# Normalized attention rows turned by DMA instead of by TensorE, and state-space tables built with fewer steps

## The reference

```python
K = einsum('chn,hnl->chl', Wc, exp(dt_Lambda[..., None] * pos))     # 32 x 128 x 1024, real part
h = concatenate([K, txt], axis=1)                                   # 32 x 205 x 1024
h = h + attention(layernorm(h), wq, wk, wv, wo)   # 32 heads of 32, 8 key/value heads, causal
h = h + ffn(layernorm(h), W_base, b_base, low-rank adapters through a Fourier transform)
```

## Time and profile before

| | us |
|---|---|
| three timed runs, median (lowest to highest) | 3075.71 (3064.27 to 3079.66) |
| the profiled execution | 3082.04 |
| its span | 3080.3 |
| busy: PE, DVE, ACT, POOL | 2781.2 (90%), 1997.8 (65%), 1094.1 (36%), 1029.9 (33%) |
| busy share of PE over the steps of attention, 400 to 1800 us | 94.5 to 96% in each 100 us |

### The profile page before, as it was taken

How to read it: one execution, slowest core, us unless ns; L and a number is a source line. 1 busy time by engine, 2 the same in 40 slices (tenths; PEclk the granted TensorE clock), 3 DMA queues, 4 the chain that set the end, 5 groups by cost and what they waited for, 6 DMA issues and landing times. The chain is left out here.

```text
span 3080.3 us, 70678 instructions
## 1 busy us (share of the span) xinstructions
PE 2781.2 (90%) x27970; PEld 2030.8 (66%) x28224; DVE 1997.8 (65%) x4642; ACT 1094.1 (36%) x2362; POOL 1029.9 (33%) x1402
## 2 busy tenths in 40 slices
PE   0847799999999999999999986699999999999999
PEld 0736698989899898989898883244444444444444
DVE  8874577787787878777787865444444444444443
ACT  3331355555555555555555565211001101100110
POOL 4631254544545454554445454011101110110110
PEclk9977899999999999999999996599999999999999
DMA  5642422222222322222222223154554455455453
GB/s 179 194 116 69 103 58 78 58 75 78 57 76 60 80 58 77 69 65 77 56 76 58 69 49 144 55 122 120 129 137 123 121 133 132 118 127 137 124 122 86
DMA packets 446040, 297.32 MB, mean 97 GB/s; under 512 B 389416, under 2 KB 407976, under 8 KB 445232
## 3 DMA queue, kind: packets, MB, share of 16 engines
q1 hardware_dynamic: 445472, 282.69, 35.7%
q10 hardware_dynamic: 240, 10.09, 1.1%
HBM read 116.36 MB, written 80.61 MB: 64 GB/s over the span
## 5 line engine op out<-in xcount | busy, mean ns | idle before, releaser
L693 POOL TENSOR_SCALAR_AFFINE_SELECT p<-p 128x256 f32<-128x256 f32 (+1 forms) x768 | 334.3, 437 | 762.0 <-ACT p L720 743.6
L805 DVE TENSOR_REDUCE mx<-psS 77x2 f32<-77x410 f32 (+1 forms) x768 | 449.3, 613 | 181.9 <-PE psS L912 110.7
L930 PE MATMUL psJ<-xth,qh 128*128 128x205 f16 x2048 | 522.0, 255 | 24.9 <-DVE qsl L813 24.7
L932 PE MATMUL psJ<-xth,ql 128*128 128x205 f16 x2048 | 518.4, 253 | 0.0
L931 PE MATMUL psJ<-xtl,qh 128*128 128x205 f16 x2048 | 516.5, 252 | 0.0
L720 ACT ACTIVATE p<-psT,escale 128x410 f32<-128x410 f32 (+1 forms) x768 | 410.4, 570 | 276.2 <-PE psT L870 256.8
L698 POOL TENSOR_TENSOR pl<-p,ph 128x410 f16<-128x410 f32 (+1 forms) x512 | 447.7, 894 | 102.5 <-ACT ph L727 95.7
L1257 POOL TENSOR_TENSOR hb<-h,bias_sb 128x1024 f32<-128x1024 f32 x52 | 122.5, 2355 | 962.4 <-DVE h L1293 962.4
L1271 ACT CAST xh<-xn 128x1024 f16<-128x1024 f32 x52 | 54.4, 1045 | 967.1 <-DVE xn L1302 967.1
L1332 PE MATMUL ps5O<-woh,ath 128*128 128x512 f16 x832 | 316.2, 380 | 26.3 <-DMA atl<-al 26.3
L1293 DVE SCALAR_TENSOR_TENSOR h<-ps5O,osc,h_in 128x512 f32<-128x512 f32 x104 | 78.1, 751 | 402.4 <-PE ps5O L1334 402.4
(11 more groups left out here) (227 smaller groups left out, 5906.9 us busy)
## 6 DMA issues: line engine op xcount, KB each, us to landing
a_in<-acat SPq DMA_DIRECT2D x52, 512.0 KB, 3.8
h_in<-hcat SPq DMA_DIRECT2D x52, 512.0 KB, 4.7
qst<-qsh SPq DMA_DIRECT2D x512, 51.2 KB, 2.1
out<-y SPq DMA_DIRECT2D x51, 512.0 KB, 3.1
hcat<-ob SPq DMA_DIRECT2D x64, 256.0 KB, 4.0
xin<-hcat SPq DMA_DIRECT2D x32, 512.0 KB
acat<-ao SPq DMA_DIRECT2D x32, 512.0 KB
qst<-qsl SPq DMA_DIRECT2D x256, 51.2 KB, 2.1
```

What stands on the lines that cost most here:

```text
L693: pool.affine_select(out=v, in_=v, compare_op=ALU.is_ge, fill=0.0, base=0, pattern=[[0, v.shape[1]], [1, w]], channel_multiplier=-1).then_ ...
L805: dve.tensor_reduce(dst, v, AX.X, ALU.max).then_inc(s_read, 1)
L930: pe.matmul(ps[:, 0:S], wh[:, k, c], xth[:, par, k, :], start=k == 0, stop=False)
L932: m = pe.matmul(ps[:, 0:S], wl[:, k, c], xth[:, par, k, :], start=False, stop=k == KC - 1)
```

## The change

In attention there is no unit x any more. A step earlier than before (b = -4 to 32; the norm is that of image b+4) DVE makes the statistics in slots 1 and 2 and the root in slot 3; ACT, in slots 4 to 7, subtracts the mean and casts a piece of 512 columns to the high part `xfh`, with two activations (`high_part`); DVE makes the low part `xfl` from it in slots 6, 7, 7 and in slot 0 of the next step (`low_part`). In that next step SP issues four DMA transposes (`turn`) of 128 and 80 rows, behind m of slot 0, or in step -1 behind the 17 loads. The loads and stores of rows move from SP's queue to ACT's; the store goes in two halves of 512 columns. DVE's division by the row sums is made for both tiles in one reciprocal and one product.

In the state-space stage the sizes are made by 36 small activations on ACT instead of two products on POOL; two phases are formed by DVE instead of four by ACT, the others come from an absolute value; all four products with the size are DVE's; and no channel's two products are added ahead of the matmul (16 matmuls a chunk).

```diff
--- before.py
+++ after.py
...
-            pool.wait_ge(ab_ok, 1)
-            for k in range(2):
-                pool.tensor_tensor(size[:, k], per_row(a[:]), per_step(iqr[:, k, :]), ALU.mult).then_inc(size_arg, 1)
-            pool.wait_ge(size_ok, 1)
-            for t in range(2):
-                pool.wait_ge(sine_ok, t + 1)
-                pool.tensor_tensor(tab[:, t], tab[:, t], size[:, 0], ALU.mult).then_inc(tab_ab, 1)
...
+            act.wait_ge(ab_ok, 1)
+            for k in range(2):
+                for r in range(LR):
+                    m = act.activation(size[:, k, :, r], a[:], ACT.Exp, scale=iqr[:, k, r:r + 1])
+                m.then_inc(size_ok, 1)
+            for la in range(LA):
+                m = act.activation(ela[:, la, :], a[:], ACT.Exp, scale=ila[:, la:la + 1])
+            m.then_inc(la_exp_ok, 1)
             act.wait_ge(args_ok, 1)
             act.activation(ex[:], args[:, 0].rearrange("p k h -> p (k h)"), ACT.Exp).then_inc(waves_ok, 1)
             act.activation(th[:], args[:, 0].rearrange("p k h -> p (k h)"), ACT.Tanh, scale=0.5).then_inc(waves_ok, 1)
-            for t in range(4):
-                act.wait_ge(base_ok, t // 2 + 1)
-                act.activation(turned[:, t], bases[t // 2], ACT.Identity, bias=phase[:, t:t + 1]).then_inc(turned_ok, 1)
+            act.wait_ge(turns_ok, 1)
+            act.activation(trig[:], turns[:], ACT.Sin, scale=TWO_PI).then_inc(waves_ok, 1)
             act.wait_ge(la_ok, 1)
-            act.activation(ela[:], fla[:, 0], ACT.Exp).then_inc(la_exp_ok, 1)
-            act.wait_ge(size_arg, 2)
-            act.activation(size, size, ACT.Exp).then_inc(size_ok, 1)
-            act.activation(trig[:], turns[:], ACT.Sin, scale=TWO_PI).then_inc(waves_ok, 1)
-            act.wait_ge(la_ok, 2)
             act.activation(tla[:], wla[:], ACT.Sin, scale=TWO_PI).then_inc(la_sin_ok, 1)
-            for t in range(4):
-                act.wait_ge(frac_ok, t + 1)
-                act.activation(tab[:, t], turned[:, t], ACT.Sin, scale=TWO_PI).then_inc(sine_ok, 1)
+            act.wait_ge(frac_ok, 1)
+            act.activation(turned[:, 1], turned[:, 0], ACT.Abs, scale=-1.0, bias=phase[:, 0:1]).then_inc(far_ok, 1)
+            act.activation(tab[:, 1], turned[:, 0], ACT.Sin, scale=-TWO_PI, bias=lag[:, 0:1]).then_inc(sine_ok, 1)
+            act.wait_ge(far_ok, 1)
+            act.activation(tab[:, 0], turned[:, 1], ACT.Sin, scale=-TWO_PI, bias=quarter[:, 0:1]).then_inc(sine_ok, 1)
+            act.wait_ge(frac_ok, 2)
+            act.activation(turned[:, 3], turned[:, 2], ACT.Abs).then_inc(far_ok, 1)
+            act.activation(tab[:, 3], turned[:, 2], ACT.Sin, scale=TWO_PI).then_inc(sine_ok, 1)
+            act.wait_ge(far_ok, 2)
+            act.activation(tab[:, 2], turned[:, 3], ACT.Sin, scale=-TWO_PI, bias=quarter[:, 0:1]).then_inc(sine_ok, 1)
...
-            for k in range(2):
-                dve.tensor_tensor(bases[k], per_row(f[:]), per_step(iqr[:, k, :]), ALU.mult).then_inc(base_ok, 1)
...
-            for t in range(4):
-                dve.wait_ge(turned_ok, t + 1)
-                chain(dve.tensor_scalar(tab[:, t], turned[:, t], ROUND, ROUND, ALU.add, ALU.subtract))
-                dve.tensor_tensor(turned[:, t], turned[:, t], tab[:, t], ALU.subtract).then_inc(frac_ok, 1)
+            for k in range(2):
+                m = dve.tensor_tensor(bases[k], per_row(f[:]), per_step(iqr[:, k, :]), ALU.mult)
+            chain(m)
+
+            chain(dve.tensor_scalar(tab[:, 0], base, phase[:, 0:1], ROUND, ALU.add, ALU.add))
+            dve.scalar_tensor_tensor(turned[:, 0], tab[:, 0], ROUND, base, ALU.subtract,
+                                     ALU.subtract).then_inc(frac_ok, 1)
+            chain(dve.tensor_scalar(tab[:, 2], base2, ROUND, None, ALU.add))
+            dve.scalar_tensor_tensor(turned[:, 2], tab[:, 2], ROUND, base2, ALU.subtract,
+                                     ALU.subtract).then_inc(frac_ok, 1)
...
-            dve.wait_ge(size_ok, 1)
-            for t in (2, 3):
-                dve.wait_ge(sine_ok, t + 1)
-                dve.tensor_tensor(tab[:, t], tab[:, t], size[:, 1], ALU.mult).then_inc(tab_cd, 1)
-            dve.wait_ge(tab_cd, 2)
+            dve.wait_ge(size_ok, 2)
+            dve.wait_ge(sine_ok, 4)
+            for t in range(4):
+                dve.tensor_tensor(tab[:, t], tab[:, t], size[:, t // 2], ALU.mult).then_inc(tab_ok, 1)
+            dve.wait_ge(tab_ok, 4)
...
-                    m = dve.tensor_tensor(es[:, ch % 2, k].rearrange("p h (q r) -> p h q r", r=LR), fast, slow, ALU.mult)
-                chain(m)
-                dve.tensor_tensor(es[:, ch % 2, 0, 0:SUMMED], es[:, ch % 2, 0, 0:SUMMED],
-                                  es[:, ch % 2, 1, 0:SUMMED], ALU.add).then_inc(e_ok, 1)
+                    dve.tensor_tensor(es[:, ch % 2, k].rearrange("p h (q r) -> p h q r", r=LR), fast, slow,
+                                      ALU.mult).then_inc(e_ok, 1)
...
-                    last = 0 if j < SUMMED else 1
-                    for k in range(last + 1):
+                    for k in range(2):
                         m = pe.matmul(ps[n % 4][:, j % 2, :], u[:, ch % 2, j].rearrange("p a c -> p (a c)"),
-                                      es[:, ch % 2, k, j, :], start=k == 0, stop=k == last)
+                                      es[:, ch % 2, k, j, :], start=k == 0, stop=k == 1)
...
-        xth, xtl = sb("xth", [P, 2, KC, S], F16), sb("xtl", [P, 2, KC, S], F16)
+        xfh, xfl = sb("xfh", [P, 2, D], F16), sb("xfl", [P, 2, D], F16)
+        xth, xtl = sb("xth", [P, 2, KC, P + TROWS], F16), sb("xtl", [P, 2, KC, P + TROWS], F16)
-        ao = sb("ao", [P, 2, 2, D])
+        ao = sb("ao", [P, 2, 2, D // 2])
...
-                if s >= 4 and has["ln"]:
-                    row.append(("x", s - 4))
...
-            return {"att": 0 <= b < B, "last": 0 <= b - 1 < B, "max": 0 <= b + 1 < B, "qkv": 0 <= b + 2 < B, "ln": 0 <= b + 3 < B, "load": 0 <= b + 4 < B}
+            return {"att": 0 <= b < B, "last": 0 <= b - 1 < B, "max": 0 <= b + 1 < B, "qkv": 0 <= b + 2 < B, "turn": 0 <= b + 3 < B,
+                    "ln": 0 <= b + 4 < B, "load": 2 <= b + 5 < B}
...
-                if has["load"]:
-                    wait(sp, pj_filled, base)
-                    load(b + 4, par)
                 if b == -1:
                     for dst, src, arrived in ahead:
                         sp.dma_start(dst, src).then_inc(arrived, 16)
-                if has["last"]:
-                    store(b - 1, nxt)
+                if has["turn"]:
+                    wait(sp, pj_filled, base)
+                    turn(0, nxt, b + 3)
+                    turn(1, nxt, b + 3)
...
+            def turn(t, to, n):
+                r, cols = ((P, slice(0, P)), (TROWS, slice(P, P + TROWS)))[t]
+                sp.wait_ge(x_lo, 4 * n + 2 * t + 2)
+                sp.dma_start_transpose(out=xth[:, to, :, cols], in_=xfh[0:r, t, :]).then_inc(xt_in[t], 16)
+                sp.dma_start_transpose(out=xtl[:, to, :, cols], in_=xfl[0:r, t, :]).then_inc(xt_in[t], 16)
...
+            pool.memset(xfh[:, 1, :], 0.0)
+            pool.memset(xfl[:, 1, :], 0.0)
...
+            def load(b, par):
+                act.dma_start(xin[:, par, 0, :], hcat[b * S:b * S + P, :]).then_inc(x_in[par], 16)
+                act.dma_start(xin[0:TXT, par, 1, :], hcat[b * S + P:b * S + S, :]).then_inc(x_in[par], 16)
+            def store(b, half):
+                c = slice(half * D // 2, (half + 1) * D // 2)
+                act.wait_ge(norm_done, 8 * b + 4 * half + 4)
+                act.dma_start(acat[b * S:b * S + P, c], ao[:, half, 0, :]).then_inc(a_out[half], 16)
+                act.dma_start(acat[b * S + P:b * S + S, c], ao[0:TXT, half, 1, :]).then_inc(a_out[half], 16)
+            def high_part(b, par, n):
+                t, h = divmod(n, 2)
+                c, r = slice(h * D // 2, (h + 1) * D // 2), T[t]
+                x = xin[0:r, par, t, c]
+                if n == 0:
+                    act.wait_ge(ln_done, b + 5)
+                if h == 0:
+                    wait(act, xt_in[t], 32 * (b + 4))
+                act.activation(x, x, ACT.Identity, bias=nmean[0:r, t:t + 1]).then_inc(centred, 1)
+                act.wait_ge(centred, 4 * (b + 4) + n + 1)
+                act.activation(xfh[0:r, t, c], x, ACT.Copy, scale=rs[0:r, 3, t:t + 1]).then_inc(x_hi, 1)
+            act.wait_ge(cleared, 1)
+            load(0, 0)
+            load(1, 1)
...
+                    if g == 3 and has["load"]:
+                        act.wait_ge(x_lo, 4 * (b + 4))
+                        load(b + 5, 1 - par)
+                    if g == 2 and has["last"]:
+                        store(b - 1, 1)
+                    if g == 6 and has["att"]:
+                        store(b, 0)
...
+                    if g >= 4 and has["ln"]:
+                        high_part(b, par, g - 4)
...
-                dve.reciprocal(rden[:, 0, :], o[:, 0, :, HD]).then_inc(rec_done, 1)
```

(66 more changed lines are left out.)

57 lines of the change are left out of this document (21 added, 36 removed).

## The result

| | before | after |
|---|---|---|
| median of 20 runs each, us | 3080.03 | 3097.01 |
| the profiled execution, us | 3082.04 | 3101.61 |
| its span, us | 3080.3 | 3099.9 |
| granted TensorE clock, mean of the span | 0.965 | 0.952 |

The change makes the kernel slower: the ratio is 1.0054, with a 95% interval from 1.0037 to 1.0071. I had forecast 3073 us and no change; 3097 lies inside the range of 3030 to 3105 but outside the forecast's own of 3057 to 3090, on the slow side. Of the 24 us between them, 4 are the median before, which three runs had put at 3075.7 and twenty put at 3080.0.

A forecast was written before the change was run, and what follows sets the result against it. PE and SP's chain of 26 issues were taken to bound attention within 0.5 us of each other. 3082.0 (profiled) - 14 (state-space stage) + 12 (attention's start) - 1 (steady steps) = 3079, 3073 as a median; range 3030 to 3105.

The forecast's parts named there:

- The state-space stage: Before attention: cheaper table work on DVE, less a longer matmul loop, together -14 us (-19 to -7).
- The four products with the sizes: State-space stage, DVE: four products instead of two, at 3.4 us each beside POOL, +6.9 us.
- The bound: Steady steps: SP's 26 issues from S (its first q issue) set slot 0's row scores, at S + 20.0 us.
- A steady step at full clock: Attention's 28 steady steps: 49.4 + 0.1 - 0.4 = 49.1 us each, -9 us in all before the clock term.
- the term for the clock: Steady steps, PE's wait for k in slot 0: 5 more clock falls, +8 us (0 to 45).
- ACT's lateness: Slots 5 and 6: exponentials 0.8 to 1.4 us late in all, taking that much of PE's 2.4 us wait.
- rival 2: Slot 0: the clock falls in most steps, 1.6 us each, 45 us instead of 8, giving 3110; chance 0.15.
- attention's start: From attention's start to step 0's row scores: slower first projection and transposes behind the loads, +12 us (6 to 16).
- two transposes at 2.19 and a landing: Attention's start: part of about 10.5 us ahead of the first projection, replacing 4.4 us of transposes and splits.
- 1 (PE's time is won): Steady steps: S comes early or the chain is faster; 3028 by half, 2985 if all; chance 0.22.
- 3: Rival: ACT bounds slots 4 to 7 through slow issues on its queue, 1 us a step, 3101; chance 0.08.
- 4: Rival: SP's idle stretch is too short, transposes over 14 us push S, 1 us a step, 3101; chance 0.05.

The follow-up runs named there:

- `root_last`: The changed kernel with the root's chain in slot 3 put behind the split of slot 3's q: 3018.4 us, ratio to before 0.9815.
- `ssm_only`: The kernel before with the new state-space stage alone: 3063.7 us, ratio to before 0.9944.
- `att_only`: The changed kernel with the old state-space stage, so the attention part alone: 3101.6 us, ratio to before 1.0076.
- `early_root`: The changed kernel with the layer norm in slots 0, 1, 2 instead of 1, 2, 3: 3067.4 us, ratio to before 0.9950.

## Why the prediction was wrong

**Right.** The state-space stage: -15.1 for -14. The four products with the sizes, and PE's first matmul:

```profile
41.12 15.90 DVE L350 TENSOR_TENSOR tab<-tab,stage 128x2048 f32<-128x2048 f32 x4
...
62.73 3.78 PE L379 MATMUL ps<-es,u 128*128 128x256 f32 x8 [62.73 <-DVE u L363]
```

against 61 forecast, and the last copy of the stage at 175.55, where it was 190.70. The total hides two misses that cancel, which is luck: the products took 15.90 us instead of 13.7 (4 x 3.4), nearer to the 3 us more that I had worked out for whole instructions in turn and then left aside, and from PE's first matmul to the last copy the stage grew by 1.8 us (111.0 to 112.8) instead of 4.5. The bound: SP's chain of 26 issues from S holds the row scores, S to R 20.1 (19.5 to 20.5 forecast), S not earlier because of the moved root (T3 + 8.5 in the step shown, 1174.28 to 1182.79), PE waiting in 27 of 28 steps, the transposes fitting SP's idle stretch (1167.94 to 1174.59, 8 us before S). A steady step at full clock: 48.92 with the wait filled, and 50.02 less 15 falls of 1.5 us over 28 steps is 49.2; forecast 49.1 (from 49.4, where the mean step before is 49.54).

**The step that failed: the term for the clock**, +8 in the sum of the steady steps, whose -1 became +13.5. I wrote "with waits of about 1.3 and a scatter of 0.7 I count 5 more falls: +8". The price of a fall was right (1.6 forecast, 1.4 to 1.7 by R to S), the count wasn't: 14 more, +21 us. Two things lie behind it as I read it. The wait was longer than I had put it, 1.8 us and not 1.0 to 1.6, since ACT's lateness was over-costed: a piece takes 1.47 us instead of the 1.3 that I took, and still PE waits for ACT only 0.28 a step; ACT seems to have more slack in slots 5 and 6 than I saw. A piece on ACT in slot 5, which answers to the earlier trace rows:

```profile
1191.07 0.72 ACT L720 ACTIVATE xin<-xin,nmean 128x512 f32<-128x512 f32 x1
1191.82 0.72 ACT L722 ACTIVATE xfh<-xin,rs 128x512 f16<-128x512 f32 x1
```

I also drew the chance of a fall from one wait in fourteen, though those of the kernel before were mostly under 1 us: only three were longer (1.40, 1.81 and 1.72), and one of these had the fall. In the changed kernel the 15 waits with a fall average 2.15 us, the 12 without 1.52. Length alone doesn't decide: a wait of 1.31 had a fall, and one of 2.03 had none; what does is open. So the time came from the mechanism of rival 2, with about half of the steps where that rival had all of them. I had given it 0.15, and had argued it down with the very lateness of ACT that did not come.

**Also missed: attention's start**, +12 forecast for the row scores of step 0 and +18.1 measured there (117.5 us from the first memset to them, then 135.6), +20.5 at the first steady R. The term "two transposes at 2.19 and a landing" was mis-sized: here a transpose issues in 1.28 to 1.35 us, not 2.19, but the last one lands 8.2 us after its issue begins, beside a load of rows that the sum did not have. ACT's wait for the constants added 3, and step 0 a further 2.5 that I did not have.

**Rivals.** 1 (PE's time is won) is false as the kernel stands, and comes true when S moves too: `root_last`. 3 and 4 are false: PE waits for ACT 0.28 a step, and S waits for no transpose.

**Open.** The changed kernel's +17 less the -17 of `ssm_only` leaves +34 for attention, `att_only` says +23, and the intervals (5 to 6 us either way) only just meet; the profiled execution of `att_only` is 31 us longer than that of the kernel before. How much the number of falls varies from one execution to the next wasn't seen: it was read in one execution of each kernel.

## What to carry to other kernels

When two chains end within a microsecond of each other, work taken off one of them buys nothing, and on TensorE it can cost: the freed time becomes a wait, and a wait of about 2 us in each step can cost 1.5 us more in clock. Move the start of the other chain first (here by one reordered block of thirteen tiny instructions, 62 us by the steps), and until then a few dead matmuls in the wait are cheaper than standing still. Judge such a wait by the granted clock in short windows behind it, not by busy shares.

## What the runs showed of the hardware

In the stage `prep_out` TensorE's clock takes one of two courses. Rows of TensorE there, in the changed kernel: the same two matmuls of 512 columns, which take 1.09 us, take 2.07 from 1945 on, with no wait ahead of them, and in `early_root` they go on at 1.12:

```profile
1941.70 1.09 PE L1121 MATMUL psA<-gt,enc 40*128 40x512 f32 x2 [1.72 <-DVE gt L1168]
...
1948.59 2.07 PE L1121 MATMUL psA<-gt,enc 40*128 40x512 f32 x2
```

```profile
1914.25 1.12 PE L1121 MATMUL psA<-gt,enc 40*128 40x512 f32 x2
```

In the 25 us from 1945 the granted clock is 0.50 with PE busy throughout, in the 25 us from 1912 of `early_root` 0.96. What follows the last steady R takes 1295.3 us in the one and 1273.7 in the other. Times of one kernel form two groups some 17 us apart: four of nine runs of `early_root` at 3047 to 3052, with a granted clock of 0.967 to 0.969 over the span, the others at 3067 to 3075, with 0.960 or 0.961. That `prep_out` makes this difference is likely, but no kernel was profiled in both groups; it is why steps are compared here, and not profiled spans. What decides between the two is open; the wait of 1.6 to 1.7 us ahead of these matmuls doesn't, since both have it.
